# A two-layer macaron network on one core: tiles of the second unit and the preparations interleaved into both early stages, and the layer norm's scale and shift made for two items at once by GpSimd

## The reference, cut to what matters

```python
x = x + 0.5 * quant_ffn(layernorm(x))        # one 512x512 matrix, dequantised from 6 bits, plus a bias
x = x + conv0(layernorm(x))                  # y = irfft(rfft(u)*rfft(K0)) + D0*u along the 512 columns
x = x + 0.5 * quant_ffn(layernorm(x))        # the same matrix again
x = x + 0.5 * swiglu_ffn(layernorm(x))       # W_down(silu(W_gate x) * (W_up x)), F = 1376
x = x + conv1(layernorm(x))
x = x + 0.5 * swiglu_ffn(layernorm(x))       # the same three matrices again
```

## Time and profile before

| | us |
|---|---|
| median of 3 runs | 924.16 (923.92 to 925.87) |
| the profiled execution, its own time | 927.85 |
| its span, first to last instruction | 926.1 |
| PE busy in the span | 883.7 (95%) |
| DVE busy | 619.8 (67%) |
| POOL busy | 368.5 (40%) |
| ACT busy | 313.7 (34%) |

### The profile page before, as it was taken

The page is one execution under the profiler, slowest core; times in us unless marked ns, Lnnn a source line. Parts: engine busy times, 40 slices in busy tenths (PEclk is TensorE's granted clock), DMA queues, the critical chain, the costliest instruction groups (busy, mean ns, idle before and its releaser), DMA issues.

```text
span 926.1 us, 11689 instructions
## 1 busy us (share of the span) xinstructions
PE 883.7 (95%) x4094; PEld 723.7 (78%) x4094; DVE 619.8 (67%) x1055; ACT 313.7 (34%) x517; POOL 368.5 (40%) x730
## 2 busy tenths in 40 slices
PE   5989998789999999999999999999999999999998
PEld 3777887567777787888888888888888778888876
DVE  6778776698888879655565786555666765444452
ACT  4423454634433434122213362222243522222121
POOL 5965466842232336332324453233243542222211
PEclk9989999999999999999999999999999999999999
DMA  8200000036766695465564665546455657666446
GB/s 332 85 0 1 1 1 1 1 129 236 272 222 224 236 337 172 150 205 156 152 177 131 203 179 173 182 130 191 151 166 162 209 144 236 203 205 205 125 140 179
DMA packets 41310, 148.27 MB, mean 160 GB/s; under 512 B 3490, under 2 KB 3746, under 8 KB 39844
## 3 DMA queue, kind: packets, MB, share of 16 engines
q0 software_dynamic: 29040, 100.93, 36.4%
q1 hardware_dynamic: 12212, 46.59, 13.7%
HBM read 117.36 MB, written 30.15 MB: 159 GB/s over the span
## 4 chain that ended last, share of the span: by engine, by line
PE 77%; DVE 12%; POOL 4%; issue 2%; ACT 2%; DMA 2%; SPq 0%; DVEq 0%; ACTq 0%; POOLq 0%
PE front L1390 14%; PE front L1392 13%; PE front L1391 13%; PE acc L1344 7%; PE acc L1345 6%; PE acc L1346 6%; PE front L451 3%; PE acc L1281 3%; PE acc L1280 3%; PE acc L1279 3%; DVE weight_operands L580 2%; DVE hidden_lo L1201 2%; DVE snapshots L1161 2%; DVE gate_up L1161 1%; DMA down_weights<-saved_down 1%
## 5 line engine op out<-in xcount | busy, mean ns | idle before, releaser
L1390 PE MATMUL front<-row_operands_hi,weight_operands 128*128 128x512 f32 x616 | 242.7, 394 | 9.0 <-DVE snapshots L1161 8.1
L1392 PE MATMUL front<-row_operands_hi,weight_operands 128*128 128x512 f32 x616 | 240.0, 390 | 0.0
L1391 PE MATMUL front<-row_operands_lo,weight_operands 128*128 128x512 f32 x616 | 239.9, 389 | 0.0
L1390 PEld LDWEIGHTS front<-row_operands_hi,weight_operands 128*128 128x128 f32 x616 | 115.6, 188 | 37.7 <-issue 10.3
L1344 PE MATMUL acc<-down_weights,hidden_hi 128*128 128x512 f32 x352 | 140.8, 400 | 3.8 <-DMA down_weights<-saved_down 2.2
L1161 DVE TENSOR_TENSOR snapshots<-front,snapshots 128x512 f32<-128x512 f32 x132 | 90.9, 689 | 78.2 <-PE front L1392 76.9
L1345 PE MATMUL acc<-down_weights,hidden_hi 128*128 128x512 f32 x352 | 138.0, 392 | 0.0
L1346 PE MATMUL acc<-down_weights,hidden_lo 128*128 128x512 f32 x352 | 137.9, 392 | 0.0
L1392 PEld LDWEIGHTS front<-row_operands_hi,weight_operands 128*128 128x128 f32 x616 | 115.6, 188 | 24.5
L1391 PEld LDWEIGHTS front<-row_operands_lo,weight_operands 128*128 128x128 f32 x616 | 115.8, 188 | 23.1
L799 POOL DMA_DIRECT2D weight_operands<-saved_weights x66 | 48.6, 736 | 185.6 <-PE front L1392 180.7
(11 more groups left out here) (166 smaller groups left out, 1351.5 us busy)
## 6 DMA issues: line engine op xcount, KB each, us to landing
weight_operands<-saved_weights POOLq DMA_DIRECT2D x33, 1280.0 KB, 6.4
down_weights<-saved_down POOLq DMA_DIRECT2D x77, 512.0 KB, 4.0
saved_weights<-weight_operands SPq DMA_DIRECT2D x11, 1792.0 KB, 8.3
weight_operands<-saved_weights POOLq DMA_DIRECT2D x33, 512.0 KB, 4.6
raw_weights<-wgu SPq DMA_DIRECT2D x11, 512.0 KB, 4.3
saved_down<-down_weights SPq DMA_DIRECT2D x11, 512.0 KB, 3.4
x_rows<-x_in SPq DMA_DIRECT2D x3, 1024.0 KB, 11.2
out<-x_rows SPq DMA_DIRECT2D x3, 1024.0 KB, 5.2
```

The lines of the kernel that those rows point to most:

```text
L1390: T.matmul(o, wh, xh, start=(j == 0), stop=False)
L1391: T.matmul(o, wh, xl, start=False, stop=False)
L1392: last = T.matmul(o, wl, xh, start=False, stop=(j == 1))
```

## The change

Four things are changed. The list of items gets another order behind the first 16 quants: eight convs (tiles 0 to 7), then q0 c8 q1 c9 q2 c10 q3 c11, then the four strings of the diff. Statistics, scale and shift, and normalising are done one item further ahead (8, 7 and 6). POOL makes scale and shift for two neighbouring items by one run of the four instructions on 128x2 operands, in odd iterations n, for items n+7 and n+8; it waits for the statistics of both. DVE does the statistics of n+8 behind the update of n instead of ahead of it. The number of products, transposes, statistics, biases and preps stays as it is. The order of the steps in POOL's iteration also stays: scale and shift first, then the bias of n+1.

```diff
-STATS_AHEAD, RSTD_AHEAD, NORM_AHEAD, XT_AHEAD, BIAS_AHEAD = 7, 6, 5, 4, 1
+STATS_AHEAD, RSTD_AHEAD, NORM_AHEAD, XT_AHEAD, BIAS_AHEAD = 8, 7, 6, 4, 1
@@ plan_items
-    for t in range(TILES):
+    for t in range(UTILES):
         light("conv", 0, t)
-    after = {UTILES - 1 + p: (p,) for p in range(UTILES)}
-    for t in range(TILES):
+    for t in range(UTILES // 2):
         light("quant", 0, t)
-        for p in after.get(t, ()):
-            prep(p)
+        light("conv", 0, UTILES + t)
+    for step in ("q4 c12 p0 q5 p1 c13", "q6 c14 p2 q7 p3 c15", "q8 q9 p4 q10 p5 q11", "q12 p6 q13 p7 q14 q15"):
+        for word in step.split():
+            if word[0] == "p":
+                prep(int(word[1:]))
+            else:
+                light({"q": "quant", "c": "conv"}[word[0]], 0, int(word[1:]))
...
@@ rstd_step
-        def rstd_step(pool, n):
-            slot = n % LN_SLOTS
-            pool.wait_ge(stats_ready, n + 1)
...
+        def rstd_step(pool, n, items=1):
+            s = slice(n % LN_SLOTS, n % LN_SLOTS + items)
+            flat = lambda t, c=0: t[:, s, c:c + 1].rearrange("p s o -> p (s o)")
+            const = lambda c: consts[:, c:c + 1].to_broadcast([P, items])
+            pool.wait_ge(stats_ready, n + items)
+            nc.gpsimd.tensor_tensor(flat(minus_mean), flat(mv), const(2), ALU.mult).then_inc(mean_negated, 1)
+            nc.gpsimd.tensor_tensor(flat(veps), flat(mv, 1), const(0), ALU.add).then_inc(eps_added, 1)
+            pool.wait_ge(eps_added, chains(n))
+            nc.gpsimd.tensor_tensor(flat(rstd), flat(veps), const(1), ALU.pow).then_inc(rstd_made, 1)
+            pool.wait_ge(rstd_made, chains(n))
+            pool.wait_ge(mean_negated, chains(n))
+            nc.gpsimd.tensor_tensor(flat(nmr), flat(minus_mean), flat(rstd), ALU.mult).then_inc(rstd_ready, items)
@@ POOL, ahead of the loop and in it
-            for n in range(XT_SLOTS, RSTD_AHEAD):
-                rstd_step(pool, n)
+            for n in range(XT_SLOTS, STATS_AHEAD, 2):
+                rstd_step(pool, n, 2)
...
-                if n + RSTD_AHEAD < PRE:
-                    rstd_step(pool, n + RSTD_AHEAD)
+                if n % 2 and n + STATS_AHEAD < PRE:
+                    rstd_step(pool, n + RSTD_AHEAD, 2)
@@ ACT, ahead of its loop
             norm_step(act, XT_SLOTS)
             den_scale()
+            for n in range(XT_SLOTS + 1, NORM_AHEAD):
+                norm_step(act, n)
@@ DVE, the loop
-                if n + STATS_AHEAD < PRE:
-                    stats_step(dve, n + STATS_AHEAD)
                 if ITEMS[n].kind == "quant":
                     dve.wait_ge(bias_added, quant_number(n) + 1)
                 if is_light(n):
                     update_step(dve, n)
+                if n + STATS_AHEAD < PRE:
+                    stats_step(dve, n + STATS_AHEAD)
```

More of the change, by code:

```diff
@@ L100, in plan_items @@
         light("quant", 0, t)
-    for t in range(TILES):
+    for t in range(UTILES):
         light("conv", 0, t)
-    after = {UTILES - 1 + p: (p,) for p in range(UTILES)}
-    for t in range(TILES):
+    for t in range(UTILES // 2):
         light("quant", 0, t)
-        for p in after.get(t, ()):
-            prep(p)
+        light("conv", 0, UTILES + t)
[5 more added lines that the diff above has]
+                light({"q": "quant", "c": "conv"}[word[0]], 0, int(word[1:]))
+    assert all(i.x_from[0] == "load" or n - next(m for m, o in enumerate(items) if o.kind != "prep"
+               and o.number == i.x_from[1] - 1) >= STATS_AHEAD for n, i in enumerate(items))
     before_units = len(items)
@@ L377, in build @@
         LOADS_OF_X = {**{t: x_first_in[t // 2] for t in range(BLK)}, **{t: x_in_sem[t // BLK] for t in range(BLK, TILES)}}
-        QUANTS_BEFORE = {0: 0, 2: TILES}
         def x_tile(t):
@@ L412, in quant_number @@
         def quant_number(n):
-            l = ITEMS[n].number
-            return l if l < TILES else l - TILES
+            return sum(1 for m in range(n) if ITEMS[m].kind == "quant")
         def stats_step(dve, n):
@@ L424, in aggregate_step, with chains @@
             nc.vector.bn_aggr(mv[:, n % LN_SLOTS, :], bnst[:, n % LN_SLOTS, :]).then_inc(stats_ready, 1)
-        def rstd_step(pool, n):
-            slot = n % LN_SLOTS
-            pool.wait_ge(stats_ready, n + 1)
[L429 to L437, removed]
+        def chains(n):
+            two = (min(n, PRE - 1) - XT_SLOTS) // 2 + 1
+            return n + 1 if n < XT_SLOTS else XT_SLOTS + two + max(0, n + 1 - PRE)
+        def rstd_step(pool, n, items=1):
[10 more added lines that the diff above has]
+            nc.gpsimd.tensor_tensor(flat(nmr), flat(minus_mean), flat(rstd), ALU.mult).then_inc(rstd_ready, items)
         def norm_step(act, n):
```

## The result

| | before | after |
|---|---|---|
| median, us | 925.01 (4 runs, 923.92 to 927.45) | 946.16 (4 runs, 945.7 to 946.9) |
| ratio to before | | 1.0212, 95% interval 1.0195 to 1.0230 |
| profiled execution, us | 927.85 | 945.70 |
| its span | 926.1 | 943.8 |
| Cauchy sums start | 54.96 | 61.75 |

The spans differ by 17.7 us: 7.45 up to product 23, 11.6 from there to the first unit product (95.9 against 84.3), and 1.4 us come back in the units. The quotient of the two medians, 1.0229, lies inside the interval of the ratio.

A forecast was written before the change was run, and what follows sets the result against it. PE, busy for 95% of the span, was taken as the bound. First stage +6.6, mixed stage +6.8 and start of the units -1 made +12.4 on 924.16, thus 936.6 us; own range 932 to 941, whole range 925 to 945.

The forecast's parts named there:

- The mechanism: New loop through DVE's aggregate, POOL's chain, bias and DVE's next iteration: 6.4 us for two items, against PE's 5.5.
- First stage: Up to the Cauchy sums: they start at 61.5 instead of 54.96, +6.5; taken as +6.6 with the convs behind.
- Mixed stage: From the transposes behind product 23 to product 55 done: 91.1 us instead of 84.3, +6.8.
- The clock: Behind PE's idle gaps: no added loss taken, with an upper end of 3 us for the new 7.1 us gap.
- Start of the units: At the first unit products: the 0.79 us wait and some of the next go, -1 us.
- (a): Rival: POOL's relief wins, -3.1 up to the Cauchy sums, about -8 in later waits, together -11: 913 us; chance 0.14.
- (b): Rival: first stage as forecast, but the mixed stage builds up no lag, -4.5; total +1.1, 925.3 us; chance 0.12.
- (c): Rival: the power on two columns doubles, 0.55 on each of some ten chains, +5: 942 to 945 us; chance 0.10.

The follow-up runs named there:

- e1: The changed kernel with POOL's bias of item n+1 ahead of the scale and shift of n+7 and n+8; 926.94 us, ratio 1.0007.
- e5: The changed kernel with the chain for two items one iteration later, in even iterations for n+6 and n+7; 918.54 us, ratio 0.9920.
- e3: The changed kernel with one scale-and-shift chain for one item (n+7) in every iteration instead of one for two; 925.64 us, ratio 1.0005.
- e6: The changed kernel with the same waits for both items, but two single chains instead of one for two; 964.21 us, ratio 1.0411.
- e12: e5 with the first chains as before the change: items 4 and 5 singly, bias 0, then 6 and 7 together; 916.84 us, ratio 0.9905.
- e9: e5 with the two preparations of a pair next to each other in the list of items; 921.17 us, ratio 0.9954.
- e2: The changed kernel with the list of items of the kernel before; chains for two and statistics behind the update stay; 934.94 us, ratio 1.0101.

## Why the prediction was right

**The time** was not well sized. The median is 946.16 for a forecast of 936.6; it lies above the forecast's own range of 932 to 941 and 1.2 us above the 945 at which the whole range ends. From one profiled execution to the other the loss is 17.7 us of span for +12.4, and the rest of the 21.15 is how far the two profiled executions lie from their medians. What was right is the direction, the mechanism and where the time goes.

**The mechanism** was as forecast: in odd iterations POOL waits for statistics that DVE makes at the end of the same iteration, with the next bias behind the wait. e1 (order of two steps), e5 (one iteration later) and e3 (one item less to wait for) each open the loop in another way and each win 19 us or more; e6 lengthens it and loses 18. The two sides of the sum had other errors:

**First stage**, forecast +6.5 at the Cauchy sums, measured +6.8 (54.96 to 61.75). Inside two errors cancel: DVE's first denominator took 0.72 instead of the 1.65 of the earlier trace rows, so POOL idled for 4.14 us ahead of its first chain in the loop (the prediction calls it the second) instead of 5.0, and each chain takes 1.40 instead of 1.18. POOL's later idle times, 0.86, 2.66 and 1.82, are those of the working. Up to product 23 it was +7.45 for +6.6; the 0.66 that came between the Cauchy sums and product 23 is not traced to a cause.

**Mixed stage**, the mis-sized term: forecast +6.8, measured +11.6 (95.9 for 91.1). The wait at p0 came 1.1 us later than worked out and was 6.46 (7.1 forecast). The period of a group, p0 to p2 and p2 to p4, was 18.3 and 18.5 instead of 16.7 and 16.6. DVE's timeline over one group, updates 32, 33, 35, then xt_lo in iteration 37, update 38:

```profile
149.71 0.69 DVE L484 TENSOR_TENSOR x_rows<-acc,x_rows 128x512 f32<-128x512 f32 x1 [2.78 <-POOL x_rows L740]
...
153.38 0.66 DVE L484 TENSOR_TENSOR x_rows<-acc,x_rows 128x512 f32<-128x512 f32 x1
...
159.50 0.69 DVE L484 TENSOR_TENSOR x_rows<-acc,x_rows 128x512 f32<-128x512 f32 x1 [2.93 <-POOL x_rows L740]
...
164.43 0.69 DVE L479 TENSOR_TENSOR xt_lo<-front,xt_hi 128x512 fp32r<-128x512 f32 x1 [0.99 <-ACT xt_hi L474]
...
167.99 0.69 DVE L484 TENSOR_TENSOR x_rows<-acc,x_rows 128x512 f32<-128x512 f32 x1 [2.78 <-POOL x_rows L740]
```

Two longer chains make 0.44 of the 1.6. Another 0.99 is the wait of xt_lo (item 41) for ACT at 164.43, and this is the step that the working left out: the loop has a second branch, through ACT. ACT normalises item 42 ahead of xt_hi of item 41, and the scales of 42 come from the very chain that POOL could start only at 161.56. ACT's timeline, and PE's transposes of item 41:

```profile
160.99 0.62 PE L462 MATMUL front<-identity,normalised 128*128 128x128 f32 x4
```

```profile
163.10 0.82 ACT L455 ACTIVATE normalised<-x_rows,minus_mean_rstd,rstd 128x512 f32<-128x512 f32 x1 [2.86 <-POOL minus_mean_rstd L448]
163.82 0.58 ACT L474 ACTIVATE xt_hi<-front 128x512 fp32r<-128x512 f32 x1
```

The transposes were done 2.2 us before xt_hi started, so PE was not what it waited for. DVE's aggregate stands behind this xt_lo, and POOL's next chain behind the aggregate. e6 confirms it: there the scales of the first item of two are ready after a single chain of 1.18 instead of 1.40, and the same wait is 0.77, shorter by just these 0.22, while PE idled longer (7.43 us at p0) and the other waits of the loop grew:

```profile
177.75 0.82 ACT L454 ACTIVATE normalised<-x_rows,minus_mean_rstd,rstd 128x512 f32<-128x512 f32 x1 [3.36 <-POOL minus_mean_rstd L447]
178.47 0.58 ACT L473 ACTIVATE xt_hi<-front 128x512 fp32r<-128x512 f32 x1
```

```profile
179.07 0.69 DVE L478 TENSOR_TENSOR xt_lo<-front,xt_hi 128x512 fp32r<-128x512 f32 x1 [0.77 <-ACT xt_hi L473]
```

e6's groups, p0 to p2 and p2 to p4, take 20.0 us: 18.28 and twice 0.97 for the longer chains, less 0.22. The second group of the changed kernel has the 0.99 too (at 182.87). The 0.15 and about 0.4 that remain in the two groups are not traced.

**The clock** did fall behind the gap at p0: it was 0.66 over 150 to 160 us, and the product and transposes from 153.43 to 158.25 took 4.8 us where warm ones take 3.2. But those 1.6 us were not paid: update 35 at 159.50 waits for POOL's bias and not for the product, and PE then idled for 4.57 us at p2. So the prediction's nothing for this term holds, and its upper end of 3 us was not needed. The Trainium skill ("TensorE: Matmul & The Clock Gate", "HAM oscillation — how this bites in real kernels") has the clock throttled by each long gap and the loss paid again behind it. The trace agrees on the throttling (0.66 here), but where another engine sets the pace behind the gap, as in this group, the loss does not appear in the time.

**Start of the units**: forecast -1, measured -1.4.

**The rivals.** (a) was not what the change did, but it was a true account of what it could do: with the loop open (e5) PE does start the Cauchy sums 3.2 us earlier than before, as worked out there (-3.1), and gains 1.8 in the mixed stage, where it said 8. (b), no lag: the mixed stretch would be 79.8; e3, e5 and e12, the new order without the loop, have 81.8 to 82.8, so even that was too low. (c), the power doubling: it takes 0.15 more, not 0.55; the whole chain takes 0.22 more.

## What to carry to other kernels

Batching two items halves the instructions of an engine, but it also makes the first wait for the second; look which of the producer's iterations the last input comes from, and what is queued behind the wait. If the producer needs what stands behind it, shift the batch by one iteration: here that turned 21 us of loss into 7 us of gain. The price of such a loop is its sum of latencies against the pace of the bound engine. Most of it can be worked out from the durations in a trace before anything is run (here +12.4 us for the 17.7 that came), but follow every engine that the late value passes: the branch through ACT, where another step stands behind the one that waits, was missed here.

## What was not expected of the hardware

The power of GpSimd on 128x2 takes 0.70 us and on 128x1 0.55, while a 128x2 multiplication takes 0.20 and a 128x1 0.19. The same DVE instruction does not always take as long: the first denominator took 1.65 us in the kernel before, 0.72 in the changed kernel and 1.05 to 1.14 in e1, e3, e5 and e9; no run shows why.

The length of a gap alone does not tell whether the granted clock falls. Between 20 and 240 us of the span there are nine gaps of PE of 3.2 us and more (in the changed kernel, e2 and e6), and over the 4 us behind each the granted clock was 0.50 to 0.67. Shorter gaps went either way. In e5 PE idled for 1.77 us both at p0 and at p2, with the clock at 1.00 before: it was 0.57 behind the first (133.37) and 1.00 behind the second (148.88). The six gaps of 1.54 of the kernel before left it at 1.00. In e3 it was 0.57 behind a gap of 2.94 us (154.02) and 1.00 behind one of 2.89 (183.09).

So a gap can cost something in one kernel and nothing in the next: e5 and e9 run the same instructions up to the Cauchy sums, and PE idled for 2.81 and 2.36 us ahead of the transposes of T4, yet from 26 to 30 us the granted clock was 1.00 in e5 and 0.63 in e9, and the Cauchy sums started at 51.8 and 53.4. A difference of 1.6 us in the first stage of one profiled execution is no result of the kernel.
